# Smaller routing pieces on VectorE behind the second maximum, q and k handled in halves, the weights' last quarters asked for first: one fused layer on one core

## The reference

```python
h = _layernorm(x) * (1 + ca) + sa
x = x + ga * attention(h)        # 16 heads of 64, rotary, causal softmax, W_out
h = _layernorm(x) * (1 + cb) + sb
x = x + gb * ffn(h)
# in ffn:
weights = softmax(h @ gate_w.T + expert_bias)
top_w, top_i = top_k(weights, 2)             # then normalised to a sum of 1
out = sum over experts e of sparse_w[e] * (gelu(h @ w_up[e].T) @ w_down[e].T)
return layernorm(out) + h
```

## Time and profile before

| what | us |
|---|---|
| median of 3 runs (1136.31 to 1139.31) | 1138.59 |
| the profiled execution's own time | 1148.27 |
| its span, first to last instruction | 1146.2 |
| PE busy | 929.1 (81%) |
| DVE busy | 868.7 (76%) |
| ACT busy | 726.3 (63%) |
| POOL busy | 546.9 (48%) |

### The profile page before, as it was taken

The page is one execution under the profiler, slowest core; times in us unless marked ns, Lnnn a source line. Parts: engine busy times, 40 slices in busy tenths (PEclk is TensorE's granted clock), DMA queues, the critical chain, the costliest instruction groups (busy, mean ns, idle before and its releaser), DMA issues. The chain is left out here.

```text
span 1146.2 us, 19703 instructions
## 1 busy us (share of the span) xinstructions
PE 929.1 (81%) x6154; PEld 669.4 (58%) x6154; DVE 868.7 (76%) x1719; ACT 726.3 (63%) x1833; POOL 546.9 (48%) x483
## 2 busy tenths in 40 slices
PE   2469999999899999989899999989985169899900
PEld 1346666666666666666666666666664158687700
DVE  6558888888888888888888888888775269777717
ACT  2247777777776777777777667777764156566604
POOL 2334445444455456455545645544563406566720
PEclk9979999999999999999999999999997579899955
DMA  6022221222222122222212321231131657566424
GB/s 207 24 64 52 56 62 47 69 48 56 62 68 63 47 65 73 56 51 74 69 47 53 85 56 47 70 77 47 45 100 43 208 193 246 187 216 224 157 79 143
DMA packets 67221, 104.22 MB, mean 91 GB/s; under 512 B 11115, under 2 KB 49912, under 8 KB 63536
## 3 DMA queue, kind: packets, MB, share of 16 engines
q1 hardware_dynamic: 61168, 91.71, 27.9%
q0 software_dynamic: 4992, 8.94, 2.4%
q10 hardware_dynamic: 960, 2.33, 0.6%
HBM read 21.09 MB, written 15.50 MB: 32 GB/s over the span
## 5 line engine op out<-in xcount | busy, mean ns | idle before, releaser
L897 ACT ACTIVATE prob<-ps,nmax 128x512 f32<-128x512 f32 (+3 forms) x512 | 264.8, 527 | 88.4 <-DVE nmax L995 86.7
L1071 POOL TENSOR_TENSOR four<-four 128x1024 f32<-128x1024 f32 x64 | 151.4, 2366 | 293.6 <-DMA four<-four 235.1
L995 DVE TENSOR_REDUCE nmax<-ps 128x2 f32<-128x1024 f32 (+3 forms) x256 | 211.0, 824 | 8.8
L1075 POOL TENSOR_TENSOR qk_lo<-four,qk_hi 128x1024 fp32r<-128x1024 f32 x64 | 152.8, 2388 | 94.9 <-ACT qk_hi L925 94.9
L816 PE MATMUL ps<-ident,prob 128*128 128x128 f32 x1280 | 190.6, 280 | 4.2 <-ACT probt L918 3.2
L816 PEld LDWEIGHTS ps<-ident,prob 128*128 128x128 f32 x1280 | 144.8, 142 | 53.5 <-ACT prob L897 23.2
L918 ACT COPY probt<-ps 128x512 f32<-128x512 f32 (+2 forms) x256 | 123.5, 513 | 76.7 <-PE ps L816 74.2
L988 DVE TENSOR_TENSOR ps<-ps,tri 128x256 f32<-128x256 f32 x256 | 109.3, 427 | 70.2 <-PE ps L795 67.8
L838 PE MATMUL ps<-probt,val 128*64 128x512 f32 (+3 forms) x1024 | 152.2, 439 | 0.0
L1467 POOL DMA_INDIRECT results<-y,to_i x92 | 101.8, 1106 | 90.3 <-DVE y L1319 61.6
L790 PE MATMUL ps<-qk_hi 64*128 64x512 f32 (+3 forms) x256 | 105.2, 411 | 48.3 <-ACT prob L897 43.6
(11 more groups left out here) (212 smaller groups left out, 2166.4 us busy)
## 6 DMA issues: line engine op xcount, KB each, us to landing
four<-four SPq DMA_DIRECT2D x256, 128.0 KB
wt<-wall SPq DMA_DIRECT2D x23, 1024.0 KB
xg<-slots SPq DMA_DIRECT2D x23, 288.0 KB
hb<-h_hi SPq DMA_DIRECT2D x64, 64.0 KB, 2.2
hb<-h_lo SPq DMA_DIRECT2D x64, 64.0 KB, 1.9
y<-results SPq DMA_DIRECT2D x8, 512.0 KB, 7.4
slots<-fill SPq DMA_DIRECT2D x8, 288.0 KB
x_all<-in_x SPq DMA_DIRECT2D x4, 512.0 KB, 10.6
```

The lines of the kernel that those rows point to most:

```text
L897: e.activation(prob[:, unit, 0:w], ps[:, bank_s(idx) + j, 0:w], ACT.Exp, bias=nmax[:, q.par, idx, j:j + 1], accum_out=den[:, q.par, 2 * i ...
L995: e.tensor_reduce(nmax[:, q.par, idx, :], ps[:, bank:bank + 2, 0:w], AX.X, ALU.max, negate=True).then_inc(v_max, 1)
L1071: e.tensor_tensor(qk, tt, ur, op=ALU.add).then_inc(g_qk, 1)
L1075: e.tensor_tensor(qk_lo[q.par][:].rearrange("p k t -> p (k t)"), qk, qk_hi[q.par][:].rearrange("p k t -> p (k t)"), op=ALU.subtract).then_ ...
```

## The change

**On VectorE,** `route_dve` moves from ahead of the first mask to behind the second maximum, ahead of `dve_ot`. The routing steps are cut anew: `r_stats` takes two tiles at c = 4 and two at c = 5; the last reduction of `r_one` moves to `r_rest`, the last two steps of that to a new `r_second` (c = 4), and the last four of `r_two` to `r_tails` (c = 6). `r_cum` leaves VectorE for GpSimd, as the first work of its slot at c = 6.

**q and k in halves:** `dve_t`, `pool_qk`, `act_hi` and `pool_lo` are now two instructions of 512 columns each, k first. A semaphore v_tk tells PE that the k half of bank W1 has been read. GpSimd waits for `dve_ot` of q2 before it adds, save in slots with c = 0.

**In the middle stage** SP asks for quarters 2 and 3 ahead of the routing's DMAs. The fills are shared out, four on SP and four on ACT's queue. The first tile's weight copy goes ahead of its rows.

The diff, cut to its core:

```diff
-        def r_stats(e, b):
+        def r_stats(e, b, half):
...
-            for t in range(TB):
+            for t in range(2 * half, 2 * half + 2):
                 e.bn_stats(st4[:, t, :], x_all[:, b * TB + t, :]).then_inc(r_st, 1)
...
+            if due(b):
+                e.wait_ge(r_sum, TB * b)
             e.tensor_tensor(hot[:, 0], rk, wide(place), op=ALU.is_equal).then_inc(done, 1)
...
+        def r_second(e, b):
+            done, tick = r_a, Count(ROUTE_A * b + 12)
+            e.wait_ge(done, tick.value)
             e.tensor_reduce(place, tied[:], AX.X, ALU.max).then_inc(done, 1)
             e.reciprocal(total, under).then_inc(done, 1)
...
+        def r_tails(e, b):
+            done, tick = r_a, Count(ROUTE_A * b + 15)
             e.tensor_tensor(share[:], hot[:, 1], wide(best), op=ALU.mult).then_inc(done, 1)
...
             done = Count(TB * b)
+            e.wait_ge(r_hot, b + 1)
+            if due(b):
+                e.wait_ge(p_pos, b)
             e.tensor_tensor(cum[:, 0], hot[:, 0, 0], hot[:, 1, 0], op=ALU.add).then_inc(r_sum, 1)
-            e.wait_ge(r_hot, b + 1)
...
+        def route_pool_first(e, i, c):
+            b = batch(i, 2)
+            if c == 6 and b is not None:
+                r_cum(e, b)
...
             def pe_turn_sum(e, q):
                 e.wait_ge(a_rep, q.n + 1)
-                e.wait_ge(v_t, min(q.n + 3, STEPS))
+                e.wait_ge(v_tk, min(q.n + 3, STEPS))
...
                 if q0.live:
-                    act_hi(e, q0)
+                    act_hi(e, q0, 1)
+                    act_hi(e, q0, 0)
...
+            def dve_t(e, q, half):
+                cols = slice(half * S, (half + 1) * S)
+                e.tensor_tensor(tt[:, cols], ps[:, W0 + half, :], turn_c[:, cols],
+                                op=ALU.mult).then_inc((v_t, v_tk)[half], 1)
...
                 if q2.live:
                     dve_store(e, q2, "2b")
-                route_dve(e, i, c)
                 if q1.live:
                     dve_mask(e, q1, 0)
                     dve_max(e, q1, 0)
                     dve_mask(e, q1, 1)
                     dve_max(e, q1, 1)
+                route_dve(e, i, c)
                 if q2.live:
                     dve_ot(e, q2)
...
+                route_pool_first(e, i, c)
                 if q2.live:
                     pool_wo(e, q2)
                 if q0.live:
-                    pool_qk(e, q0)
-                    pool_lo(e, q0)
+                    if q2.live and i and c:
+
+                        e.wait_ge(v_ot, q2.n + 1)
+                    pool_qk(e, q0, 1)
+                    pool_qk(e, q0, 0)
+                    pool_lo(e, q0, 1)
+                    pool_lo(e, q0, 0)
                 route_pool(e, i, c)
...
+                    for q in range(2, 4):
+                        e.wait_ge(s_wlo, q - 1)
+                        sp_raw(e, q)
+                    for i, c in LATE:
+                        route_sp(e, i, c)
+                    mark_ends(e, 0, NX // 2)
                     e.wait_ge(v_table, 1)
...
                         if j == 0:
+                            e.wait_ge(s_wlo, 4)
+                            copy_weights(e, j, col)
                             e.wait_ge(d_xs, 16 * 2 * NT)
                             e.wait_ge(d_fill, 16 * (NX + 1))
...
                     high(e, 2)
                     high(e, 3)
+                    mark_ends(e, NX // 2, NX)
                     act_x(e, 0)
```

More of the change, by code:

```diff
@@ L373, in r_rest @@
             e.tensor_scalar(under, under, 1.0, None, ALU.add).then_inc(done, 1)
-            e.wait_ge(done, tick.after(2))
+        def r_second(e, b):
+            done, tick = r_a, Count(ROUTE_A * b + 12)
+            e.wait_ge(done, tick.value)
             e.tensor_reduce(place, tied[:], AX.X, ALU.max).then_inc(done, 1)
@@ L484, in route_dve @@
             b, a = batch(i, 2), batch(i, 1)
-            if c == 4 and a is not None:
-                r_stats(e, a)
+            if c in (4, 5) and a is not None:
+                r_stats(e, a, c - 4)
             if b is None:
@@ L494, in route_dve @@
                 r_rest(e, b)
+            if c == 4:
+                r_second(e, b)
             if c == 5:
@@ L497, in route_dve @@
             if c == 6:
-                r_cum(e, b)
+                r_tails(e, b)
             if c == 7:
@@ L749, in pe_qk @@
                     e.wait_ge(v_t, n)
+                    e.wait_ge(v_tk, n)
                 if due(n - 2):
@@ L918, in act_store, with act_hi @@
                 e.copy(dst, src).then_inc(a_ev, 1)
-            def act_hi(e, q):
+            def act_hi(e, q, half):
                 n = q.n
-                e.wait_ge(g_qk, n + 1)
+                e.wait_ge(g_qk, 2 * n + 2 - half)
                 if due(TB * (n - 1)):
                     e.wait_ge(p_s, TB * (n - 1))
-                e.copy(qk_hi[q.par][:].rearrange("p k t -> p (k t)"), qk).then_inc(a_hi, 1)
+                e.copy(qk_hi[q.par][:, half, :], qk[:, half * S:(half + 1) * S]).then_inc(a_hi, 1)
             def act_v(e, v):
@@ L1038, in dve_slot @@
                 if q0.live:
-                    dve_t(e, q0)
+                    dve_t(e, q0, 1)
+                    dve_t(e, q0, 0)
                 if q2.live:
                     dve_store(e, q2, "2b")
-                route_dve(e, i, c)
                 if q1.live:
@@ L1063, in pool_wo, with pool_qk @@
                                 ga[:, q.b, :], op=ALU.mult).then_inc(g_wo, 1)
-            def pool_qk(e, q):
-                n = q.n
+            def pool_qk(e, q, half):
+                n, cols = q.n, slice(half * S, (half + 1) * S)
                 e.wait_ge(v_t, n + 1)
@@ L1069, in pool_qk, with pool_lo @@
                 if due(n):
[L1070 to L1076, removed]
+                    e.wait_ge(g_lo, 2 * n)
+                e.tensor_tensor(qk[:, cols], tt[:, cols], ur[:, cols], op=ALU.add).then_inc(g_qk, 1)
+            def pool_lo(e, q, half):
+                e.wait_ge(a_hi, 2 * q.n + 2 - half)
+                e.tensor_tensor(qk_lo[q.par][:, half, :], qk[:, half * S:(half + 1) * S], qk_hi[q.par][:, half, :],
+                                op=ALU.subtract).then_inc(g_lo, 1)
             def pool_slot(e, i, c):
                 q0, _, q2 = pairs(i, c)
+                route_pool_first(e, i, c)
                 if q2.live:
@@ L1332, in dve_residual, with copy_weights, mark_ends @@
                 e.tensor_tensor(x_all[:, n, :], x_all[:, n, :], gated[:], op=ALU.add).then_inc(v_g, 1)
+            def copy_weights(e, j, col):
+                e.dma_start(wt[j % 3][:].rearrange("p k i -> p (k i)").bitcast(F32),
+                            wall[:].rearrange("p x k i -> p (x k i)")[:, bass.ds(col, 4 * I)].bitcast(F32))\
+                    .then_inc(d_wt[j % 3], 16)
+            def mark_ends(e, first_, last):
+                e.wait_ge(v_ended, 1)
+                for x in range(first_, last):
+                    end = e.value_load(ended[0:1, x:x + 1], min_val=x * REGION, max_val=x * REGION + B * S)
+                    e.dma_start(xs[bass.ds(end, S), :].rearrange("(p t) f -> p t f", t=TB),
+                                fill[:].unsqueeze(1).to_broadcast([P, TB, ROW])).then_inc(d_fill, 16)
             with nc.Block() as block:
```

28 lines of the change are left out of this document (11 added, 17 removed).

## The result

The changed kernel takes 1102.55 us (median of 4 runs, 1101.81 to 1105.63) against 1138.95 for the kernel before, run beside it. The ratio is 0.969, 95% interval [0.9665, 0.9714]: 36.4 us less. The forecast was 1107. The profiled execution took 1102.95 with a span of 1101.1.

A forecast was written before the change was run, and what follows sets the result against it. No engine is full; two successive stretches, DVE with ACT, then PE, set each attention slot. Attention −22.5 and middle stage −9 give −31.5 us: 1138.6 to 1107 us, forecast's own range 1099 to 1114, overall 1096 to 1127.

The forecast's parts named there:

- The first stretch one for one: Attention slot, opening to first maximum on DVE and ACT: anything put ahead of the first maximum lengthens every slot equally.
- The term: 31 routing instructions moved behind the second maximum, 0.16 us each: 5.0 us won in eight slots, less 0.3 at c = 7.
- The cover: DVE idle time behind the second maximum plus PE's later use of `dve_ot`: about 1.25 us, hiding all moved routing.
- The cosine split at 0.10 a slot: DVE's cosine product as two instructions of 512 columns: costs 0.10 us in every slot's first stretch, 0.8 in eight.
- The "slack" of the earlier transposes: PE's transposes of the sums may start one half earlier; said to add only slack, no time won.
- Late transfers, 0.3 in eight: Transfers landing later than 6.9 us after the opening no longer fit in some slots: 0.3 us lost per eight slots.
- POOL's wait and the halves: POOL waits for `dve_ot`, 6.9 us after opening; halves take 5.2, low part ready at 12.1, PE wants it at 12.15.
- The circle of rivals 1 and 2: Loop from low part through `dve_ot` sets the slot: period 12.1, 1118 us (chance 0.15); or 12.8 and slower (0.05).
- First pairs and last slots: Attention's ends: the first 14 pairs pay 1.4 us and win about 0.8; the last four slots win about 1.5.
- The middle stage: Between attention and first expert matmul: reordered DMAs start PE earlier, minus 9 us taken, range −12 to −2.
- My third rival: Middle stage gives nothing, as POOL's queue replaces SP's and `low` holds scatters; attention alone, 1116 us; chance 0.12.
- POOL's queue and the subtractions: Middle stage: `r_cum` behind POOL's scatters, and DVE's long subtractions beside the last scatters: 2 us cost, bounds 0 and 9.

## Why the prediction was right, point by point

**The first stretch one for one: right, and shown.** The mask stands 2.87 after the opening at c = 5, the slots with c = 1, 3, 4 and 5 take 11.69 to 11.77, and the routing put back gives 12.38 again. The term was 5.0 us less 0.3 in eight slots; with the cosine's 0.8 taken off, 3.86; measured 4.48. Over all 48 slots the mask's mean start fell from 3.57 to 2.99 after the opening, 4.65 in eight slots: one for one. The cover held too: `ot` starts at 6.01 in the mean (6.21 before), and PE's output projection waits for it once, 0.9 us.

The term was too small at c = 2 by 0.31 and at c = 7 by 0.37, too large at c = 3 by 0.19. At c = 2 the six instructions had put the mask 1.23 later (4.04 after the opening, 2.81 without), 0.2 each and not 0.16. For c = 7 I took 0.3 of the moved work as hidden behind ACT's lateness, from one pair with a wait of 1.12. It was the longest of six: PE's mean wait there was 0.70 before and is 0.80 now. The mask comes 0.46 sooner and the slot is 0.45 shorter, so nothing was hidden.

**The cosine split at 0.10 a slot: mis-sized.** It was 0.07 by its own rows (1.24 for two halves against 1.17 in the earlier trace rows), and at the mask 0.07 at most and 0.015 in the mean, with `ot` 0.24 sooner in return. The "slack" of the earlier transposes was a gain.

**Late transfers, 0.3 in eight: right in kind, too large.** In the three pairs of 48 where the transfer lets the addition start only 7.19 to 7.23 after the opening, the slot takes 11.91 to 11.94, 0.25 more than its like. That is about 0.1 in eight.

**POOL's wait and the halves: right, with more room.** I put the low part at 12.1 and it is at 11.75: `ot` starts at 5.97 and not at 6.2, and the four halves take 5.01, not 5.2. The circle of rivals 1 and 2 has 0.37 us to spare; with whole pieces it closes, and the slots lose 18.6 us. The wait itself stood in my sum as a cost that the halves pay back. I had named what it keeps apart, but put no price on that and had no rival about it. The runs show it as the larger half of the matter: without it 31 us are lost, all of the gain and more.

**First pairs and last slots: −0.5 and 0.0** instead of +0.6 and −1.5; together 0.4 off.

**The middle stage: −7.4 for −8.7.** The order of SP's list is worth 9.6 by the run with the old one, and the counts on POOL cost about 2. The error has two terms that nearly cancel. POOL's queue and the subtractions cost 4.8 us and not 2: the request goes out 39.4 after the end of attention, and 34.6 was the time without them. And the rows land 2.7 after the request instead of the 4.5 that I took between 1.9 and 7.4. My third rival has its mechanism confirmed (scatters over 0.96 beside L1202, counts behind the scatters), at half the price that it needed.

**Sum.** −22.5 was −27.3, −9 was −7.4: 3.2 us too little in all, of 36.4. The remaining 1.7 lies between two profiles and two medians, and I don't assign it.

## What to carry to other kernels

Before small work is moved under another engine's stretch, ask which long instruction runs there and what both read: here the same move is worth 24.5 us with a wait that keeps the two apart, and costs 7.7 without it. A wait that delays an engine off the critical path can be paid back by halving that engine's instructions, since its consumer may begin at half. And when a stall in one queue is removed, read the next entry of each queue in order: SP's list decided both the middle stage's gain and the failure of the run that held the subtractions back.

## What the runs showed of the hardware that I had not expected

GpSimd's indirect DMA instructions are held by a VectorE subtraction with two SBUF inputs (my third rival had this as possible). Beside the 2 × 2.29 us of L1202 two scatters take 2.86 and 1.78 us, and 2.70 and 1.89; with the second pair of subtractions moved away, the second eight scatters take 0.95 to 0.98. The Trainium skill, "SBUF — State Buffer", section "Who interferes with whom", supposes the opposite for the descriptors of GpSimd's DMAs, and these rows differ from it. An indirect DMA also reads its addresses (`slot_of`) from SBUF, and no run here separates that read from the writing of the descriptors.

The exclusion goes by whole instructions and takes the shorter one along: products and comparisons of 0.19 us became 0.97 to 1.30 beside a half of 1.28, and up to 2.40 beside a whole addition of 2.37. A scalar step of 4 columns (L375), which has one tensor as input, became 1.28. So what is left of the neighbour's instruction, not one's own length, is the price. Reductions, reciprocals and statistics ran beside the same addition undisturbed (0.17 to 0.28).

Cutting a VectorE product of 1024 columns from PSUM in two cost 0.07 us (1.24 against 1.17), where the durations of single instructions allow up to 0.21. 288 KB of rows landed in 2.7 to 3.1 us where the transfer ahead of them had been asked for about 6 us earlier, in 5.2 us with a copy of 1024 KB asked for 0.8 us ahead, and in 6.9 us behind two quarters of the weights.
